# Graph attention over 64 channels: where a group's exponentials and turn stand, and how PSUM is cut

## What is computed

```python
def _gat(x, src, dst, W, a_src, a_dst, b, concat, n):
    H, C = a_src.shape
    h = (x @ W).reshape(n, H, C)
    s_src = (h * a_src).sum(-1)
    s_dst = (h * a_dst).sum(-1)
    e = jax.nn.leaky_relu(s_src[src] + s_dst[dst], NEG_SLOPE)
    m = jax.ops.segment_max(e, dst, num_segments=n)
    ex = jnp.exp(e - m[dst])
    denom = jax.ops.segment_sum(ex, dst, num_segments=n)
    alpha = ex / (denom[dst] + 1e-16)
    out = jax.ops.segment_sum(h[src] * alpha[:, :, None], dst, num_segments=n)
    out = out.reshape(n, H * C) if concat else out.mean(axis=1)
    return out + b
...
h = _gat(x, src, dst, We1, as_e1, ad_e1, b_e1, True, n)        # a: 16 channels
enc = _gat(h, src, dst, We2, as_e2, ad_e2, b_e2, False, n)     # b: 32
h2 = _gat(enc, src, dst, Wd1, as_d1, ad_d1, b_d1, True, n)     # c: 16
dec = _gat(h2, src, dst, Wd2, as_d2, ad_d2, b_d2, False, n)    # d: 64
```

## Time and profile before

| | us |
|---|---|
| median of three runs | 10316.04 |
| the runs | 10315.06 to 10322.73 |
| span of the profiled execution | 10328.9 |
| gathers of layer d, first to last start | 5594.1 to 7395.8 |
| gathers of layer b, first to last start | 2762.5 to 3935.5 |

### The profile page before, as it was taken

How to read it: one execution, slowest core, us unless ns; L and a number is a source line. 1 busy time by engine, 2 the same in 40 slices (tenths; PEclk the granted TensorE clock), 3 DMA queues, 4 the chain that set the end, 5 groups by cost and what they waited for, 6 DMA issues and landing times. The chain is left out here.

```text
span 10328.9 us, 112817 instructions
## 1 busy us (share of the span) xinstructions
PE 5861.0 (57%) x40667; PEld 5155.4 (50%) x40667; DVE 3843.7 (37%) x8462; ACT 2213.6 (21%) x5853; POOL 5595.9 (54%) x5805
## 2 busy tenths in 40 slices
PE   2444534555366665455554666666569999942232
PEld 1333424444255554344443666666549999932222
DVE  4444523333344443344443334433332222232233
ACT  0000012222033331122221333333311111111111
POOL 7666466666666665666666666666540000036665
PEclk7666656676578876566665788888759999975555
DMA  4555342221133331333322444444318988821111
GB/s 157 174 178 172 79 50 56 54 56 42 48 99 100 99 99 28 93 96 104 100 70 76 120 125 122 124 123 125 81 61 341 353 339 333 334 94 24 23 24 23
DMA packets 445732, 1238.85 MB, mean 120 GB/s; under 512 B 162082, under 2 KB 235683, under 8 KB 401971
## 3 DMA queue, kind: packets, MB, share of 16 engines
q1 hardware_dynamic: 208148, 741.90, 20.6%
q0 software_dynamic: 237024, 489.72, 19.4%
HBM read 1101.15 MB, written 127.51 MB: 119 GB/s over the span
## 5 line engine op out<-in xcount | busy, mean ns | idle before, releaser
L1247 PE MATMUL ps<-pool 128*106 128x128 f32 (+2 forms) x19344 | 3019.8, 319 | 1618.8 <-issue 1018.0
L1247 PEld LDWEIGHTS ps<-pool 128*106 128x106 f32 (+2 forms) x19344 | 2770.2, 195 | 1823.2 <-issue 1202.1
L1205 ACT ACTIVATE ACC<-ps 72x256 f32 (+1 forms) x2418 | 1010.1, 418 | 2530.0 <-remote 1632.8
L470 POOL DMA_INDIRECT ACC<-t,ACC x416 | 392.5, 944 | 1647.2 <-DVE ps L1776 1447.6
L752 POOL DMA_INDIRECT cnt_d<-pool x806 | 832.0, 1032 | 534.2 <-issue 221.5
L1274 POOL DMA_INDIRECT pool<-d_h,srcT_s x806 | 770.8, 956 | 582.1 <-PE ps L1247 296.7
L489 PE MATMUL ps<-pool 128*65 128x128 f32 (+1 forms) x2392 | 468.5, 373 | 1037.8 <-DVE pool L478 600.3
L456 DVE TENSOR_TENSOR ACC<-ACC,ps 65x128 f32 (+1 forms) x1612 | 454.0, 282 | 1443.8 <-remote 1022.6
L1274 POOL DMA_INDIRECT pool<-a_h,srcT_s x806 | 778.3, 966 | 383.1 <-issue 229.8
L1274 POOL DMA_INDIRECT pool<-b_h,srcT_s x806 | 762.7, 946 | 411.6 <-issue 210.2
L1274 POOL DMA_INDIRECT pool<-c_h,srcT_s x806 | 764.1, 948 | 396.9 <-issue 229.3
(11 more groups left out here) (298 smaller groups left out, 5964.3 us busy)
## 6 DMA issues: line engine op xcount, KB each, us to landing
ACC<-cnt_d SPq DMA_DIRECT2D x186, 1600.0 KB, 8.8
pool<-cnt_d SPq DMA_DIRECT2D x94, 1600.0 KB, 8.9
cnt_d<-pool SPq DMA_DIRECT2D x28, 3200.0 KB
ACC<-key_d SPq DMA_DIRECT2D x31, 1664.0 KB
ACC<-key_d SPq DMA_DIRECT2D x25, 2048.0 KB
pool<-seg_d SPq DMA_DIRECT2D x100, 129.0 KB
cnt_d<-pool POOLq DMA_INDIRECT x806
pool<-a_h,srcT_s POOLq DMA_INDIRECT x806
```

Source lines behind the costliest of these rows:

```text
L470: g.indirect_dma_start(out=gb[b][:, k, :], out_offset=None, in_=table, in_offset=bass.IndirectOffsetOnAxis(ap=idx[:, c:c + 1], axis=0)).th ...
L1205: a.activation(win[:, 0:NPL, bass.ds(reg, 128)], pl[0].rearrange("p (i c) -> p i c", c=128), ACT.Copy).then_inc(*(tile_out if last else A) ...
L1247: mm = t.matmul(o, gbr[:, tile % RT, M * i:M * i + M], oh, start=True, stop=True)
```

## The change

Four places in gat. In layer d the PSUM is cut into three sets of one tile: tile n uses banks 2(n mod 3) for its 512 columns and 2(n mod 3) + 1 for its 128. BACK goes from 15 to 10, the turn of probabilities behind the eleventh tile of a group; EXP from 11 to 8, the exponentials behind the ninth. TURN stays. And in layer d VectorE writes both one-hot halves behind the logits, where the first stood ahead of them. Layers a, b and c keep their order. Behind line 1156 all line numbers grow by one.

```diff
--- before.py
+++ after.py
@@ -928,10 +928,10 @@
             mxc = M * (NPL - 1) + MX
             nout = 128 if dst is None else C
 
-            S, R = {16: (4, 3), 32: (2, 3), 64: (2, 2)}[C]
+            S, R = {16: (4, 3), 32: (2, 3), 64: (1, 3)}[C]
 
             PIECE = 128 // C
-            TURN, BACK, EXP = (7, 15, 11) if C == 64 else (-1, 11, 7)
+            TURN, BACK, EXP = (7, 10, 8) if C == 64 else (-1, 11, 7)
             w = wl[0:kin, 0:HC]
             av, dv = wl[:, 512:512 + HC], wl[:, 1024:1024 + HC]
             ht = dram(name + "_h", (NP, RW))
@@ -1153,10 +1153,11 @@
             def vector_edge_prepare(gi):
                 hs = halves(gi)
                 vector_edge_scores(gi)
-                vector_edge_onehot(*hs[0])
+                if layer < 3:
+                    vector_edge_onehot(*hs[0])
                 vector_edge_logits(gi)
-                if len(hs) > 1:
-                    vector_edge_onehot(*hs[1])
+                for half in hs[0 if layer == 3 else 1:]:
+                    vector_edge_onehot(*half)
 
             def vector_pass():
                 vector_edge_prepare(0)
@@ -1185,7 +1186,7 @@
                     return [ps[2 * (st % R) + k // 2][0:M, 256 * (k % 2):256 * (k % 2) + 256]]
                 if C == 32:
                     return [ps[2 * (st % R) + k][0:M, 0:384]]
-                return [ps[2 * (st % R) + k][0:M, 0:512], ps[4 + st % R][0:M, 128 * k:128 * k + 128]]
+                return [ps[2 * (st % R)][0:M, 0:512], ps[2 * (st % R) + 1][0:M, 0:128]]
 
             def scalar_slots(tile, reg):
                 last = tile % S == S - 1 or tile == NT - 1
```

## The result

| | us |
|---|---|
| kernel before, median of 4 runs beside it | 10319.39 (10315.06 to 10324.23) |
| changed kernel, median of 4 runs | 10196.16 (10192.71 to 10202.04) |
| ratio | 0.9878, interval 0.9864 to 0.9892 |
| spans of the profiled executions | 10328.9 before, 10193.6 after |

The account below looks back on a forecast made before the run. GpSimd, at 28.9 us a group, would bound layer d once TensorE's gap closed. Of 336 us of its waits 193 would stay, so 143 off 10,316 gives 10,173 us, range 9,995 to 10,310.

Parts of the forecast that it names:

- The 336 us: GpSimd's waits for TensorE in layer d, less issue time: the most the change could win, 6.7 us a group.
- The turn: Layer d: turning behind tile 11, exponentials behind tile 9, shrinks TensorE's 5.8 us gap to 0.7, winning 5.1 us a group.
- The share kept: GpSimd's waits for TensorE in layer d that stay after the change: 193 us of 336.
- The slope from a and b: 28 us of waits per added product a tile from layer a to b, giving 221 us kept in d.
- The clock: Layer d's first two tiles run at half clock after TensorE's gap; closing it could save 2.1 us a group.
- The rival built on it: TensorE's clock stays low in layer d, 35.8 us a group: no change, 10,316 us; chance 0.03.
- The sets: Three one-tile PSUM sets in layer d: -67 to +85 us over TensorE's 77 waits for ScalarE, taken as 0.
- The one-hots: Layer d's first one-hot behind the logits adds 1.22 us, at most 61 us, taken as covered but for 0.7 us.
- GpSimd's floor: Rival: lateness goes with the gap and GpSimd never waits in layer d, 9,980 us; chance with cases near it 0.12.
- The gap did not survive: Rival: turned probabilities come 6.5 us late, TensorE waits 6.2 us; whole, 10,316 us, chance 0.08; partly, 10,230 to 10,295, 0.13.
- The slower case: Rival: gap survives, TensorE stops sooner on three PSUM tiles, ScalarE stands; some 67 us slower, 10,383 us; chance 0.14.
- The held-back results: Layer d: TensorE's results seem held back, some 6.5 us in one group, while GpSimd issues, until it runs dry.

Follow-up runs that it names:

- s4_pause: Changed kernel with a small GpSimd iota behind each gather of layer d, which the next gather waits for; 9073.96 us, ratio 1.009, results seen at once.
- p1_sets: Kernel before with only the three PSUM sets of one tile in layer d; 8988.84 us, ratio 0.9996, results seen at once.
- r2: Changed kernel with the 344 scatters moved from between layer d's gathers to behind the layer; 10258.39 us, ratio to kernel before 0.9848.
- r3: Kernel before with the 344 scatters moved from between layer d's gathers to behind the layer; 10520.32 us, ratio 1.010.
- p2: Changed kernel with the two PSUM sets of two tiles put back; 8981.33 us, ratio to kernel before 0.9988, results seen at once.
- r1_after: The changed kernel run again unaltered beside the kernel before, results late; 10273.98 us against 10416.49, ratio 0.9857.
- r4_narrow: Changed kernel gathering 264 floats a row in place of 520 in layer d, as many transfers; 10273.49 us in one run, results late.
- p3: Changed kernel with the first one-hot ahead of the logits again; 8976.53 us, ratio to kernel before 0.9985, results seen at once.
- s2: Repeat of p2, the changed kernel with two PSUM sets of two tiles; 8979.22 us, ratio to kernel before 0.9986, results seen at once.
- s3: Repeat of p3, the changed kernel with the first one-hot ahead of the logits; 8976.48 us, ratio to kernel before 0.9981.

## Why the prediction was right, and where it was off

**What bounds.** Shown. GpSimd's own work was put at 28.9 us a group; 29.17 is what it takes where it never waits, and s4_pause shows that its queue is the bound. The 336 us were the right pool to draw from: the gathers lasted 1,801.7 us before and 1,468.0 in p1_sets, 334 us less.

**The turn.** r2 and r3 show the change as a whole: 4.65 us a group between them, 5.1 forecast for the gap. That it is the turn and not the sets that closes the gap is shown by p1 and p2, where results come at once; where they come late it is argued from there. In the changed kernel L1148 no longer holds TensorE (6.2 us, under 100 forecast).

**The share kept.** The term of the sum was 193 us; 264.3 less 188 times 0.306 are 207, and with the five stops under "issue" 217. r1_after kept 287.9 less 61 = 227. The slope from a and b had said 221 and was near; the middle that I took between it and layer b was too low by 24 us. Either way it is an extrapolation that held, not a mechanism that was shown.

**The step that was off: how waits became time.** I let the whole of 336 less 193 = 143 us off come out of the gathers. They got 115.0 us shorter (1,801.7 to 1,686.7). 24 of the 28 us that are missing were kept as waits (217 us and not 193), and 4 lie in the instructions themselves, 2.7 in the gathers (mean 960 ns against 956) and 1.3 in the scatters. Against this stands a gain that the sum did not have. From the last gather to the first L1499 (L1500 after) of layer d's last products it took 104.7 us before and 85.3 after. No gather is left to hide a gap there, and TensorE's two last ones fell away whole, 9.2 us of these 19. The rest is not resolved; the mean granted clock of this stretch was 0.68 before and 0.72 after. The two gaps stand in the timeline of TensorE of the kernel before:

```profile
7435.72 11.52 PE L1247 MATMUL ps<-pool 128*106 128x128 f32 x80 [5.30 <-DVE pool L1148]
...
7460.39 8.47 PE L1247 MATMUL ps<-pool 128*106 128x128 f32 x60 [3.94 <-DVE pool L1148]
```

That sums the profiled spans: 115 in the gathers, 2 ahead of them, 18 to 19 behind, 135.3 us in all. The medians differ by 123, since the profiled execution of before lay high, as the prediction had said of it. So the forecast of 143 owes part of its nearness to luck: it gave the gathers 28 us too much and the tail behind them 18 us too little.

**The clock.** This reading was wrong. I tied the low clock to the 5.82 us gap and let 2.1 us a group come back with it. The gap is gone and stretches at 0.50 remain, now behind two short waits for ScalarE; over 5660 to 7350 us the mean granted clock is 0.82, from 0.81, and the 8,060 records of products of layer d last 315 ns on average where they lasted 312. The Trainium skill, "TensorE: Matmul & The Clock Gate", section "A second HAM failure mode: psum-queue depth-cycling", has such short idles between bursts make the clock swing, and here the trace agrees with it. The trace of before could have warned: behind its wait of 2.94 us for ScalarE the granted clock was 0.50 too, from 6401.80 to 6406.40. But in p2_turn, with sets of two tiles, 30 records also ran slow behind 8.55 us of idling. The error stayed outside the sum, because GpSimd bounds and TensorE had some us to spare. The rival built on it (no change, 10,316) put every tile at the low clock. At a mean of 0.82 the full clock held for most of the time, and TensorE did not become the bound.

**The sets.** "I take 0" held for the time where results come at once (0.9996 and 0.9998). The bounds of -67 to +85 us were too narrow for the wait itself: TensorE's wait for ScalarE grew by 217.5 us. It stops behind three tiles where it stopped behind four, 195 times and not 77. GpSimd's kept waits came out 24 us above the forecast; how much of that the sets put there, no run shows. Where results are late its effect was not measured apart.

**The one-hots.** Taken as covered, and no run contradicts it: in p2_turn, with both one-hots behind the logits, the gap is closed all the same. The cover seems to have been named wrongly, which is argued and not tested. It is the wait of L1106 for gathered rows (34.7 us in 4 places before, 303.6 in 50 after), which the prediction did not foresee and which takes up what VectorE loses elsewhere. With the gap closed TensorE and VectorE run as far ahead as the rows let them.

**The rivals.** GpSimd's floor was not reached by closing the gap; it appears with results at once, and then in both kernels. The gap did not survive. The slower case needed the turn's result later than 5.1 us. In the group shown it was 6383.10 less 6379.01, about 4.1 us late, and the gap paid.

**The held-back results.** They stayed, and DVE's wait for the scores with them (574.4 us). They go with the late condition and not with bytes (r4_narrow). They do not wait without exception for GpSimd to run dry, as ScalarE's start at 6392.94 shows. What makes the condition stays open, and so does whether GpSimd's issuing causes the lateness or only ends together with it, as the pause was not seen where it would tell.

## What to carry to other kernels

First find the engine that bounds a stage, and count how long it waited, and for what; a gap elsewhere is worth that part of it and no more, so the change gave 1.2% where GpSimd had waited for the gap, and closing the gap gave 0.1 to 0.2% (in p2, p3, s2, s3) where it had not. Behind the last item of the bounding queue another engine sets the pace, and there a gap pays whole. To close a gap that is a round trip through two engines, ask for the answer while work for several tiles is still queued behind the question, and then read completion by the engines that wait, not by the ends of TensorE's records.

## What the runs showed of the hardware

- The kernel before took 10,416 us in one series and 8,993 in another on the same chip, with a mean granted clock of 0.736 in the one and 0.773 in the other, for reasons that no run shows. In the second, the semaphore updates of TensorE in the attention layers stand 0.01 us behind its records; where results are late, the turned scores of the groups shown were seen 6.5 us late before (6393.62 to 6400.12) and 2.8 us late after (6404.61 to 6407.39).
- In the group shown late results came to VectorE, ScalarE and GpSimd within 0.2 us of one another (6383.10, 6383.14, 6383.29), 1.4 to 1.6 us after GpSimd's last transfer; others reached ScalarE between two of its transfers (6380.28, and 6392.94 before). Half the bytes changed nothing (290.2 against 287.9 us of waits); without the scatters the stops were shorter (median 1.36 against 1.72 us).
- GpSimd gives one indirect transfer per 1.25 us with nothing to wait for; a 0.25 us instruction between two of them costs only 0.12.
- The granted clock was 0.50 behind two idles of TensorE of 1.0 to 1.6 us with one tile at the full clock between, as it was behind one of 5.8 and behind one of 2.9.
